# Summing four of the sixteen softmax groups with strided reduces on VectorE, and multiplying all odd value groups of layer 1 as f32r halves

## What is computed

```
# layer 0
g_x     = einsum('ic,bcn->bni', g_w, xf) + g_b            # 64 inner channels
theta_x = einsum('ic,bcn->bni', theta_w, xf) + theta_b
phi_x   = einsum('ic,bcn->bin', phi_w, xf) + phi_b
f       = softmax(einsum('bni,bim->bnm', theta_x, phi_x), axis=-1)
y       = einsum('bnm,bmi->bni', f, g_x)
x       = W_w @ y + W_b + x
# layer 1
q, k, v = Wq x + bq, Wk x + bk, Wv x + bv                 # 128 channels
attn    = softmax(einsum('bnc,bcm->bnm', q, k) / sqrt(128), axis=-1)
x       = x + attn @ v
```

## Time and profile before

| | |
|---|---|
| median of 3 runs | 3421.43 us (3421.1 to 3422.05) |
| profiled execution, its own time | 3420.95 us |
| its span in the trace | 3419.1 us (1.85 us lie around it) |
| granted TensorE clock, mean | 0.992 |
| PE busy | 3332.7 us, 97% |
| DVE busy | 2098.5 us, 61% |
| ACT busy | 1671.9 us, 49% |
| POOL busy | 2965.6 us, 87% |

### The profile page before, as it was taken

The page is one execution under the profiler, slowest core; times in us unless marked ns, Lnnn a source line. Parts: engine busy times, 40 slices in busy tenths (PEclk is TensorE's granted clock), DMA queues, the critical chain, the costliest instruction groups (busy, mean ns, idle before and its releaser), DMA issues.

```text
span 3419.1 us, 46664 instructions
## 1 busy us (share of the span) xinstructions
PE 3332.7 (97%) x13124; PEld 2109.5 (62%) x13124; DVE 2098.5 (61%) x3028; ACT 1671.9 (49%) x2241; POOL 2965.6 (87%) x1366
## 2 busy tenths in 40 slices
PE   8999999999999989999999998999999999999998
PEld 5555566666555556666655555666665555566665
DVE  5555576766555556676755555667675555667674
ACT  4555444444455544444445554444444555444444
POOL 6899698988899969898989996988898999688897
PEclk9999999999999999999999999999999999999999
DMA  1000000000000000000000000000000000000000
GB/s 46 19 15 19 22 16 16 19 19 13 19 19 18 16 23 16 16 22 16 19 13 19 19 16 23 19 13 22 16 19 13 19 19 16 19 13 16 13 13 10
DMA packets 32038, 61.73 MB, mean 18 GB/s; under 512 B 3536, under 2 KB 3536, under 8 KB 31824
## 3 DMA queue, kind: packets, MB, share of 16 engines
q1 hardware_dynamic: 31824, 59.23, 5.7%
HBM read 42.44 MB, written 16.78 MB: 17 GB/s over the span
## 4 chain that ended last, share of the span: by engine, by line
PE 87%; issue 4%; POOL 4%; DVE 3%; ACT 1%; DVEq 0%; DMA 0%; ACTq 0%; POOLq 0%; SPq 0%
PE rough L388 15%; PE acc_out L461 14%; PE acc_out L445 13%; PE scores L410 7%; PE scores L413 7%; PE scores L415 6%; PE scores L419 6%; PE scores L416 6%; POOL sums L281 3%; DVE piece_max L786 2%; PE acc_out L431 2%; PE acc_out L433 2%; PE acc_out L432 2%; PE rough L370 2%; PE acc_out L482 1%
## 5 line engine op out<-in xcount | busy, mean ns | idle before, releaser
L281 POOL TENSOR_TENSOR sums<-sums,probs 128x1024 f32<-128x1024 f32 x886 | 2115.6, 2388 | 146.5 <-ACT probs L708 106.6
L786 DVE TENSOR_REDUCE piece_max<-rough 128x1 f32<-128x512 f32 x2024 | 1310.0, 685 | 644.6 <-PE rough L388 641.9
L803 DVE TENSOR_TENSOR probs<-scores,shift_rows 128x1024 f32<-128x1024 f32 x512 | 626.7, 1224 | 566.5 <-PE scores L419 539.4
L708 ACT ACTIVATE probs<-scores 128x1024 f32<-128x1024 f32 x512 | 520.1, 1025 | 673.3 <-PE scores L413 654.7
L701 ACT ACTIVATE probs<-probs 128x1024 f32<-128x1024 f32 x512 | 539.7, 1054 | 500.8 <-DVE probs L803 500.6
L906 POOL TENSOR_TENSOR p_lo<-probs,p_hi 128x1024 fp32r<-128x1024 f32 x192 | 459.0, 2391 | 187.8 <-ACT probs L701 187.6
L461 PE MATMUL acc_out<-probs,v_vals 128*128 128x512 f32 x1280 | 603.4, 594 | 0.0
L415 PE MATMUL scores<-qry_a,k_hi 128*128 128x512 f32 x1024 | 505.8, 494 | 0.0
L445 PE MATMUL acc_out<-probs,g_vals 128*64 128x512 f32 x2048 | 495.0, 605 | 0.0
L410 PE MATMUL scores<-qry_a,phi_a 128*128 128x512 f32 x1024 | 431.6, 422 | 0.0
L700 ACT ACTIVATE p_hi<-probs 128x1024 fp32r<-128x1024 f32 x192 | 203.5, 1060 | 441.4 <-DVE probs L803 383.1
(11 more groups left out here) (96 smaller groups left out, 2958.6 us busy)
## 6 DMA issues: line engine op xcount, KB each, us to landing
x_q<-x SPq DMA_DIRECT2D x32, 256.0 KB, 2.7
x_res<-x SPq DMA_DIRECT2D x32, 256.0 KB, 3.0
mid<-mid_new SPq DMA_DIRECT2D x32, 256.0 KB, 2.2
x_q<-mid SPq DMA_DIRECT2D x32, 256.0 KB, 2.8
x_res<-mid SPq DMA_DIRECT2D x32, 256.0 KB, 3.1
out<-result SPq DMA_DIRECT2D x32, 256.0 KB, 2.3
x_kv<-x SPq DMA_DIRECT2D x24, 256.0 KB, 2.7
probs<-x SPq DMA_DIRECT2D x4, 512.0 KB, 7.1
```

The source lines that it names most:

```text
L281: eng.tensor_tensor(sums[:, parity], sums[:, parity], probs[:, s % P_BUFS], ALU.add).then_inc(s_plus, 1)
L786: nc.vector.reduce_max(piece_max[:, t, c:c + 1], src, AX.X).then_inc(s_reduced, 1)
L803: nc.vector.tensor_tensor(probs[:, s % P_BUFS].rearrange("p (h c) -> p h c", c=QB), scores[:, s % 2].rearrange("p (h c) -> p h c", c=QB), ...
```

## The change

VectorE now sums groups 8 to 11 (`SUMMED`) by itself, in four instructions of 128 queries each (`sum_part`), and GpSimd adds only the other twelve. Groups 8 to 11 lie in the first four buffers of `probs`. Each instruction reads eight values for each query, 2048 bytes apart, and writes their sum: 128 x 1024 numbers in, 128 x 128 out. One part stands in slot 13 after the pieces, one in slot 14, two in slot 15 (`SUM_PARTS_AT`). The fold has a second step, `total + part_sum`. The four buffers that held groups 8 to 11 are given free by a new semaphore `s_part`. Groups 7 and 15 join `HALVED`. The last value matmul of a block, which is now a halved one, carries the `stop` mark.

```diff
-HALVED = (1, 3, 5, 9, 11, 13)
+HALVED = (1, 3, 5, 7, 9, 11, 13, 15)
+SUMMED = (8, 9, 10, 11)
+SUM_PARTS_AT = {13: 1, 14: 1, 15: 2}
...
-    ADDS = GROUPS - 1
+    ADDS = GROUPS - 1 - len(SUMMED)
...
         def probs_free(eng, g, s):
 
             eng.wait_ge(s_used, g * GROUPS + s + 1)
-            eng.wait_ge(s_plus, added(g, s - P_BUFS) if s >= P_BUFS else g * ADDS + s + 1)
+            if s >= P_BUFS:
+                eng.wait_ge(s_plus, added(g, s - P_BUFS))
+            elif s + P_BUFS in SUMMED:
+                eng.wait_ge(s_part, g + 1)
+            else:
+                eng.wait_ge(s_plus, g * ADDS + s + 1)
...
             eng.tensor_tensor(total[:], sums[:, parity, 0:QB], sums[:, parity, QB:GC],
-                              ALU.add).then_inc(s_fold, 1)
+                              ALU.add).then_inc(s_half, 1)
+            eng.wait_ge(s_half, g + 1)
+            eng.wait_ge(s_part, g + 2)
+            eng.tensor_tensor(total[:], total[:], part_sum[:], ALU.add).then_inc(s_fold, 1)
 
         def add(eng, layer, g, parity, s):
 
-            if s == 0:
+            if s == 0 or s in SUMMED:
                 return
...
+            def sum_part(g, n):
+
+                dve.wait_ge(s_whole, whole_of(g, SUMMED[-1]))
+                if n == 0 and not (isinstance(g, int) and g == 0):
+                    dve.wait_ge(s_fold, g)
+                at = slice(n * P, (n + 1) * P)
+                src = probs[:, 0:len(SUMMED)].rearrange("p a (h c) -> p c (a h)", c=QB)[:, at]
+                last = nc.vector.tensor_reduce(part_sum[:, at], src, AX.X, ALU.add)
+                if n == SUB - 1:
+                    last.then_inc(s_part, 1)
...
+                    for _ in range(SUM_PARTS_AT.get(s, 0)):
+                        sum_part(st.g, part)
+                        part += 1
```

More of the change, by code:

```diff
@@ L90, in build @@
     assert BLOCKS == 8 and LAG == 3
-    ADDS = GROUPS - 1
+    ADDS = GROUPS - 1 - len(SUMMED)
+    assert SUMMED[0] == P_BUFS and sum(SUM_PARTS_AT.values()) == SUB
     TPC = QB // KT
@@ L139, in build @@
         total = sb("total", [P, QB])
+        part_sum = sb("part_sum", [P, QB])
         o_sb = sb("o_sb", [P, QB])
@@ L193, in build @@
         s_fold = sem("s_fold")
+        s_half = sem("s_half")
+        s_part = sem("s_part")
         s_den = sem("s_den")
@@ L247, in added @@
         def added(g, s):
-            return g * ADDS + max(s, 1) + P_BUFS
+            return g * ADDS + (max(s, 1) if s < SUMMED[0] else s - len(SUMMED)) + P_BUFS
         def whole_of(g, s):
@@ L279, in add @@
                 return
-            eng.wait_ge(s_plus, added(g, s - 1))
+            eng.wait_ge(s_plus, added(g, SUMMED[0] - 1 if s == SUMMED[-1] + 1 else s - 1))
             eng.tensor_tensor(sums[:, parity], sums[:, parity], probs[:, s % P_BUFS],
@@ L432, in halved_values @@
                     mm(acc_out[:, parity], hi, p_lo[:, n, at], start=False, stop=False)
-                    last = mm(acc_out[:, parity], lo, p_hi[:, n, at], start=False, stop=False)
+                    last = mm(acc_out[:, parity], lo, p_hi[:, n, at], start=False,
+                              stop=s * TPG + h == TILES - 1)
                 last.then_inc(s_used, 1)
@@ L841, in _ @@
             for free, n in ((s_reduced, 1), (s_whole, 2), (s_plus, P_BUFS),
-                            (s_den, 1), (s_used, P_BUFS), (s_done, 2), (s_stored, 16),
+                            (s_den, 1), (s_part, 1), (s_used, P_BUFS), (s_done, 2), (s_stored, 16),
                             (s_mid, 32), (l_phi, 1), (l_k, 1)):
@@ L864, in block_program @@
                 m = 0
+                part = 0
                 for s in range(GROUPS):
```

## The result

The changed kernel takes 3609.1 us (median of 4 runs, 3604.57 to 3613.7) against 3421.49 us for the kernel before on the same chip (4 runs, 3421.1 to 3422.05): 1.055 times as long, 95% interval 1.0536 to 1.0563. I had forecast 3415; my rival of a doubled sum price gave 3614. The profiled execution took 3610.19 us, its span is 3608.4.

A forecast was written before the change was run, and what follows sets the result against it. PE was taken to bound the kernel (87% of the chain). From 3420.95 us, -11.2 (group 15), +3.1 (diagonal), +2.9 (turns), -1.2 (last block) gave 3414.55, so 3415.0 us with the runs' median offset; forecast 3409 to 3420, range 3404 to 3441.

The forecast's parts named there:

- rival of a doubled sum price: VectorE's strided sums take 2.29 us each, delaying diagonals, next pieces and turns: 199 us more, 3614 us; chance 0.15.
- the price of a sum on DVE: Each VectorE sum of 1024 numbers takes 1.22 us, 1.14 from start to start; four make 4.6 us a block.
- break-even price: The sum's price on VectorE at which the 6.4 us gain is used up: 1.40 us.
- The rule that I had quoted against the change: For the sums' 2048-byte steps: a different 16-byte SBUF line at each access pays a penalty of unstated size.
- Group 15 halved: Multiplied in slot 2 of the next block: 0.36 us saved behind 31 layer-1 blocks, 11.2 us.
- Group 7 saves nothing: In slot 10 PE waits for DVE by what halving saves; the rival of 11.2 us more had chance 0.05.
- The diagonal late by 0.11: In slot 13 of layer-0 blocks the first sum delays the diagonal: 0.11 us lost in 28 blocks, +3.1 us.
- Turns +0.72: At the four turns the second fold step isn't hidden: 0.72 us each, +2.9 us; the sums are hidden.
- The last block: PE's 2.44 us wait for a p_lo shrinks until the sums' chain on DVE takes over: -1.2 us, bounds 0 and -2.4.
- GpSimd's relief: 3.6 us less GpSimd work per layer-1 block, 8.4 per layer-0 block; gains nothing, as PE hardly waits for POOL.
- The collision with GpSimd: Rival: each VectorE sum waits about 1 us for a GpSimd add, giving about 3600 us; chance 0.04.

The follow-up runs named there:

- experiment 4: The changed kernel with all four sums reading at unit step (other numbers added up): 3412.47 us, ratio 0.9975 to the kernel before, a sum 1209 ns.
- experiment 6: The changed kernel with sums reading two neighbouring numbers, then a step of 1024 bytes (other numbers): 3414.81 us, a sum 1210 ns.
- experiment 3: The changed kernel with its four sums reading at steps of 4, 8, 16 and 2048 bytes: 3485.81 us (a single run).
- experiment 2: The kernel before with all eight odd groups halved, GpSimd still adding all sixteen, no sums on VectorE: 3420.02 us, ratio 0.9995.
- experiment 7: The changed kernel with VectorE's strided sums on groups 8 and 9 only, GpSimd adding 10 and 11 again: 3410.26 us, ratio 0.997.
- experiment 8: The changed kernel with contiguous additions of groups 8 and 9 in slot 15 instead of the strided sums: 3592.63 us, ratio 1.0503 to the kernel before.
- experiment 10: The changed kernel with the first sum behind the diagonal in layer-0 blocks: 3635.66 us, ratio 1.0629 to the kernel before.
- experiment 9: The changed kernel with four contiguous additions of the same four groups in place of the strided sums: 3615.05 us, ratio 1.0564 to the kernel before.

## Why the prediction was wrong, step by step

**The step that failed is the price of a sum on DVE.** I took 1.22 us (bounds 1.2 and 1.54) from rows whose reads were all contiguous or from PSUM. It was 2.00 us with the read of one number every 2048 bytes, and 1.21 us with the same count of numbers and results read by unit step or in pairs (experiments 4 and 6). The break-even price had been worked out as 1.40 us. The rule that I had quoted against the change was right. The Trainium skill, "Advanced Engine Details and Errata", section Memory Cachelines, has lines of 16 bytes in SBUF and wants at least two hits on one. The traces agree: the price jumps between steps of 8 and 16 bytes (experiment 3; none in between was run), and pairs are free (experiment 6). The dearer step of 32 bytes is not explained by it. The size of the penalty, which it doesn't give, is 0.79 us on 1024 numbers, 0.77 ns for each number read alone. From 512 to 1024 numbers the strided sum went from 1.082 to 1.997 us, 1.79 ns a number, against 1.02 contiguous. I gave this rival 0.15 and left it outside the range. With a rule that names the case, an access that meets its condition for every number, and no row that speaks against it, it should have had at least even odds, and the range should have reached it.

**A second term stood at nothing without a reason: TensorE's clock.** Neither the sum nor a rival had it. The new waits let it fall in 12 of the 24 layer-0 distances and in 11 of the 27 layer-1 ones, 1.65 us each, and over the whole span it is worth up to 57 of the 189 us (the estimate above). The unit-step kernel, without these waits, has none of these falls; its mean clock is 0.990.

**The doubled-price rival had the right path, and its time came out by luck.** It put 3.88 us on a layer-0 block, 2.39 net on a layer-1 block, and 3614 in all (3609). Measured were 3.49 and 2.36 on the mean, but 2.66 and 1.94 where the clock held. With the measured price, 0.78 us above 1.22, the prediction's own terms give 0.78 + (3 x 0.78 - 0.48) + 0.11 = 2.75 us for a layer-0 block, near the 2.66. Two errors met: the price was 1.64 times and not double, and the working knew nothing of the clock.

**The other terms**, read from the unit-step kernel of experiment 4, in which only the price is put right:
- Group 15 halved, 0.36 a block: in the changed kernel slot 2 of a layer-1 block is 2414.77 to 2417.97, 3.20 us as forecast. A plain layer-1 block went from 59.90 to 59.52 in the unit-step kernel.
- Group 7 saves nothing: right. Slot 10 now has the wait that slot 12 had (below), and the 0.38 of a plain block is little more than group 15's 0.36.
- The diagonal late by 0.11: 44.05 to 44.17 us, right.
- Turns +0.72: right where it was put. At the first turn the denominators' matmul (L482, now L497) starts 3.01 us after the last matmul group ahead of it (390.42 to 393.43), 2.27 before (390.08 to 392.35). Into and out of the turn taken together, since the first sum moves the mark, a turn takes +1.5 us on the mean, 3 us more in all than forecast. The clock accounts for it: the second turn, with the same 10.2 us at the lower level as before, takes +0.77, the other three, with 13.6 to 13.7 us, +1.5 to +2.0. The windows over the first two turns of the unit-step kernel (0.81 in both before):

```profile
393.00:420.00 27.00, 19.34 (x63) 12.55 (x64) 15.01 (x24) 10.67 (x19) 5.68 (x4) 0.75 0.12 39
1239.00:1266.00 27.00, 19.51 (x64) 12.51 (x64) 15.18 (x24) 11.57 (x19) 7.56 (x5) 0.81 0.14 42
```

- The last block: -2.1 behind the last diagonal instead of -1.2. The wait moved from p_lo to the sums' chain on DVE (2.29 us at the denominators), as described.
- Missed, in favour: the one slow block per image (60.4 to 61.1) is gone, and the last image's blocks get shorter by 0.84 and not 0.36 us on the mean, together some 6 us. I had put GpSimd's relief at nothing. In experiment 2, without the relief, the slow blocks stay, so it isn't nothing.

Slots 10 and 12 on PE of the changed kernel:

```profile
2447.11 0.50 PE L402 MATMUL rough<-k_hi,qry_a 128*128 128x512 f32 x1 [0.26 <-DVE piece_max L801]
...
2455.53 0.50 PE L402 MATMUL rough<-k_hi,qry_a 128*128 128x512 f32 x1 [0.26 <-DVE piece_max L801]
```

**The collision with GpSimd** does not touch the sums, as I argued. In the unit-step kernel every sum runs beside a GpSimd instruction and all lie between 1207 and 1214 ns. In the changed kernel four sums met no GpSimd instruction at all and still took 1925 to 1932 ns. The strided sums do scatter, from 1924 to 2066 ns; by what is open. The Trainium skill, "SBUF — State Buffer", section "SBUF: two separate sides", has a VectorE instruction outside the two-port modes and a GpSimd one that reads SBUF lock each other out only when the VectorE one has two SBUF inputs. The traces agree: the sums of experiment 7, with one input, take 1.10 us where no GpSimd instruction runs beside them and 1.08 where one does, and the additions of experiment 8, with two inputs, wait.

## What to carry to other kernels

Before a reduction is moved to VectorE over a rearranged view, look at its innermost step: at least two neighbouring f32 numbers in a row, or count 1.8 ns a number instead of 1.0; if the layout can't give that, take fewer numbers, as many as the idle time in front of the next instruction on the path holds. An addition of two SBUF tiles is no way out beside GpSimd's own adds: here each could wait for a whole one. An engine at 71% can carry the loss of a kernel: what counted was the length of its queue between two instructions that PE waits for. And a new wait on PE can cost more than its length, so read the granted clock behind it before the loss is put down to the wait alone.

## What the runs showed of the hardware that I had not expected

- VectorE's strided f32 read: 1.21 us for 1024 numbers at steps of 4 or 8 bytes and in pairs 1024 bytes apart, 1.93 to 2.05 us on the mean at 16, 64 to 512 and 2048 bytes, 2.17 at 32.
- VectorE's addition of two SBUF tiles of 128x1024 beside a busy GpSimd: 3.04 us on the mean where one alone takes 1.23, and GpSimd's adds got longer too (2388 to 2441 and 2580 ns).
- TensorE's clock after two waits of about 0.65 and 1.40 us: held in 12 of 24 layer-0 distances, fell to its lower level in the other 12, at 1.65 us each. After one wait of 1.5 to 1.9 us it fell in 11 of 27 (layer 1 of the changed kernel), after one of 2.4 us in 24 of 24 (experiment 10), after one of 2.64 to 2.70 us in 2 of 20 (experiment 9), after one of mostly 2.9 to 3.1 us in 26 of 27 (experiment 8).
